# Cross-attention block on one core: the two copies of each next x tile moved to other places in the order of ScalarE and VectorE

## What is computed

```python
q = layer_norm(query, ln1_g, ln1_b)
qh, kh, vh = q @ wq + bq, context @ wk + bk, context @ wv + bv   # 16 heads of 32
scores = where(allowed, einsum('bqhd,bkhd->bhqk', qh, kh) / sqrt(32), -inf)   # causal
o = einsum('bhqk,bkhd->bqhd', softmax(scores), vh)
x = query + (o @ wo + bo)
h = layer_norm(x, ln2_g, ln2_b)
out = x + gelu(h @ w1 + b1) @ w2 + b2
```

## Time and profile before

| | us |
|---|---|
| median of 3 runs | 3094.44 |
| lowest, highest | 3094.41, 3095.11 |
| the profiled execution, its own time | 3096.19 |
| span of its trace | 3094.5 |
| mean granted clock of TensorE, share of full | 0.982 |

### The profile page before, as it was taken

The page is one execution under the profiler, slowest core; times in us unless marked ns, Lnnn a source line. Parts: engine busy times, 40 slices in busy tenths (PEclk is TensorE's granted clock), DMA queues, the critical chain, the costliest instruction groups (busy, mean ns, idle before and its releaser), DMA issues. The chain is left out here.

```text
span 3094.5 us, 52560 instructions
## 1 busy us (share of the span) xinstructions
PE 2965.2 (96%) x17576; PEld 2408.6 (78%) x17576; DVE 1520.4 (49%) x4100; ACT 1153.1 (37%) x2958; POOL 459.1 (15%) x432
## 2 busy tenths in 40 slices
PE   6999999999999999999979999999999999999999
PEld 5777877778777777777758888888888888888887
DVE  4766666666676666766634333322333322333322
ACT  3655566555666565655622111111111111111111
POOL 1222122211222112222112000000000000000000
PEclk9999999999999999999979999999999999999999
DMA  5766676666666666666522111100111100111100
GB/s 133 122 113 102 111 107 111 115 110 108 107 108 119 112 102 115 103 119 110 89 85 82 41 41 41 41 9 32 41 41 41 41 31 10 41 41 41 41 27 14
DMA packets 123695, 231.89 MB, mean 75 GB/s; under 512 B 10752, under 2 KB 10752, under 8 KB 123648
## 3 DMA queue, kind: packets, MB, share of 16 engines
q1 hardware_dynamic: 123648, 231.28, 37.5%
HBM read 97.02 MB, written 33.55 MB: 42 GB/s over the span
## 5 line engine op out<-in xcount | busy, mean ns | idle before, releaser
L710 ACT ACTIVATE sm<-sm,mins 128x128 f32<-128x128 f32 (+3 forms) x1024 | 571.7, 559 | 606.4 <-DVE mins L574 603.6
L574 DVE CUSTOM_DVE_ANT_0 sm<-bank_s,mask 128x128 f32<-128x128 f32 (+3 forms) x1024 | 480.7, 488 | 451.2 <-PE bank_s L425 440.5
L1146 ACT ACTIVATE g_sb<-bank_f,b1s 128x512 f32<-128x512 f32 x256 | 176.2, 688 | 1173.1 <-PE bank_f L956 1173.1
L1058 DVE CAST g_hi<-g_sb 128x512 fp32r<-128x512 f32 x256 | 113.0, 441 | 866.9 <-ACT g_sb L1146 866.9
L437 PE MATMUL bank_t<-ident,sm 128*128 128x128 f32 x2560 | 424.1, 281 | 53.5 <-ACT pT L520 34.1
L437 PEld LDWEIGHTS bank_t<-ident,sm 128*128 128x128 f32 x2560 | 305.8, 143 | 156.9 <-issue 76.6
L954 PE MATMUL bank_f<-hT_hi,w_hi 128*128 128x512 f32 x1024 | 407.6, 398 | 1.6 <-DVE hT_lo L1052 1.6
L954 PE MATMUL bank_o<-w_hi,g_hi 128*128 128x512 f32 x1024 | 408.0, 398 | 0.0
L956 PE MATMUL bank_f<-hT_hi,w_lo 128*128 128x512 f32 x1024 | 406.7, 397 | 0.0
L955 PE MATMUL bank_f<-hT_lo,w_hi 128*128 128x512 f32 x1024 | 406.4, 397 | 0.0
L956 PE MATMUL bank_o<-w_hi,g_lo 128*128 128x512 f32 x1024 | 406.3, 397 | 0.0
(11 more groups left out here) (108 smaller groups left out, 4486.5 us busy)
## 6 DMA issues: line engine op xcount, KB each, us to landing
stack<-st_hi SPq DMA_DIRECT2D x256, 256.0 KB, 5.6
xt<-in_x SPq DMA_DIRECT2D x32, 1024.0 KB, 5.3
stack<-st_lo SPq DMA_DIRECT2D x128, 256.0 KB, 7.2
c_raw<-in_ctxT SPq DMA_DIRECT2D x64, 256.0 KB, 6.0
x_scratch<-xt SPq DMA_DIRECT2D x64, 256.0 KB, 2.0
xn<-x_scratch SPq DMA_DIRECT2D x16, 1024.0 KB, 7.7
xr<-x_scratch SPq DMA_DIRECT2D x16, 1024.0 KB, 5.6
out<-xr SPq DMA_DIRECT2D x64, 256.0 KB, 2.1
```

The costliest lines, as they stand in the source:

```text
L574: op = V.tensor_tensor_reduce(sm[:, n % SLOTS_S, off:off + w], bank_s[n % BANKS_S][:, off:off + w], mask[:, 512 - w:512], 1.0, 0.0, ALU.ad ...
L710: op = A.activation(row, row, ACT.Exp, bias=mins[:, g % 2, c:c + 1], scale=-1.0, accum_out=sums[:, g % 2, c:c + 1])
L1058: V.tensor_copy(g_hi[:, f % RING_H, :], g_sb[:, f % 2, :]).then_inc(g_hi_ok, 1)
L1146: A.activation(g_sb[:, f % 2, :], bank_f[f % 2][:], ACT.Gelu, bias=b1s[:, f:f + 1], scale=1.0).then_inc(gelu, 1)
```

## The change

On ACT, `x_high` is called at the start of the step in which its X job ends, ahead of `exponential`, instead of behind exponential, move and `o_high`. On DVE, `x_low` is called right behind `mask_and_max` of the step in which the job ends, ahead of the move, instead of at the end of the following step. The conditions of the waits, the buffers and PE's order stay as they are. The prologue's four X tiles are not touched.

```diff
--- before.py
+++ after.py
@@ -627,6 +627,9 @@
                     g, k = divmod(n, TG)
                     if not it.tail:
                         mask_and_max(it, n)
+                    for job, jg in it.ended(n):
+                        if job[0] == "X":
+                            x_low(it, job, jg, it.b + 1)
                     if (n > LAG and not it.tail or n <= LAG and not it.first) and not act_moves((n - LAG - 1) % TG):
                         move_tile(dve, V.tensor_copy, it, n - LAG - 1)
                     beside_previous = g < NG and not (it.first and g == 0) and n < len(it.steps)
@@ -645,8 +648,6 @@
                                 normalise(it.b + 1, t)
                     for job, jg in it.ended(n - 1):
 
-                        if job[0] == "X":
-                            x_low(it, job, jg, it.b + 1)
                         if job[0] in "QK":
                             qk_low(it, job, jg, it.b * NG + (jg + 1))
                     for job, jg in it.ended(n):
@@ -742,6 +743,9 @@
             def body(it):
                 for n in range(len(it.steps)):
                     g, k = divmod(n, TG)
+                    for job, jg in it.ended(n):
+                        if job[0] == "X":
+                            x_high(it, job, jg)
                     if not it.tail:
                         exponential(it, n)
                     if (n > LAG and not it.tail or n <= LAG and not it.first) and act_moves((n - LAG - 1) % TG):
@@ -752,8 +756,6 @@
                         if k == (O_HIGH_LATE if g == 1 else O_HIGH_AT):
                             o_high(it, g - 1)
                     for job, jg in it.ended(n):
-                        if job[0] == "X":
-                            x_high(it, job, jg)
                         if job[0] in "QK":
                             qk_high(it, job, jg, it.b * NG + (jg + 1))
                         if job[0] == "V":
```

## The result

| | before | after |
|---|---|---|
| median, us | 3094.78 (4 runs, 3094.41 to 3096.00) | 3068.83 (4 runs, 3062.19 to 3069.66) |
| profiled execution, us | 3096.19 | 3068.40 |
| span, us | 3094.5 | 3066.7 |
| mean granted clock | 0.982 | 0.989 |

The ratio is 0.9911, with a 95% interval of 0.9894 to 0.9928: 26 us faster, where 13 were forecast.

What follows compares the result with a forecast made beforehand. PE was taken to bound the kernel except for some 9 us per batch, where DVE is the limit. 5.3 us from the shorter chain plus 7.7 from the clock gave 13.0: median 3081.4 from 3094.44, range 3066 to 3093.

Steps and rivals of the forecast that it cites:

- the clock: Behind PE's wait ahead of the Q product: 5 of 14 clock drops saved, 5 x 1.54 = 7.7 us.
- DVE is the limit in the x steps, PE elsewhere: Four x steps per stage A batch: DVE busy 9.08 of 9.40 us, PE 6.23; whole batches: PE 90.88 of 95.32.
- The chain of starts: Steps 7 to 11, worked out by start-to-start distances: Q product at 1449.42 instead of 1449.77.
- The gain per batch in the x steps: X3's wait goes, the wait for step 10's move takes nearly all its place: 0.35 per batch, 5.3 us in 15.
- The new wait for ScalarE's copy: DVE, step 10: waits 0.84 us for ACT's copy of X3, with the move of step 10 queued behind.
- The price of one: A drop from 2.4 to 1.2 GHz where PE is dense costs 1.54 us, from batches of 95.32 and 93.78.
- rival (a): Behind the Q product's wait the clock stays as it is: two close waits work like one, or only matmuls count; 3089.1, chance 0.23.
- Rival (b): Behind the Q product's wait all drops go, as a wait below 1 us never brings one; 3067.5, chance 0.17.
- Rival (c): Slower: a doubled wait before step 8's transposes brings a drop inside the x steps; up to 3112.2, chance 0.10.
- Rival (d): ACT holds up X3's copy 0.2 to 0.4 more, clock gives little: no effect that can be told; 3091 to 3096, chance 0.13.

Runs made afterwards that it cites:

- two kernels with filler: Kernel before, with six matmuls or twelve transposes of overwritten result added into PE's wait ahead of the Q product: 3076.17 and 3076.69 us beside 3095.81.
- kernel with VectorE's half alone: Changed kernel with ScalarE's copies back behind the exponential, only VectorE's low-half subtractions staying early: 3187.47 us, ratio 1.0291.
- four further orders: Changed kernel with VectorE's subtractions back: 3093.56; X3's low half back: 3105.84; step 10's move first: 3056.08; all low halves behind moves, ScalarE's step 9 move earlier: 3046.22.

## Why the prediction was right and wrong

The step that failed is one term of the sum, the clock: 7.7 us were forecast for it where some 20 came. The rest of the working held, in the parts below.

*DVE is the limit in the x steps, PE elsewhere: right.* With the same instructions, the order of VectorE's queue alone made the kernel before 92 us slower and the changed kernel another 13 us faster (3068.78 to 3056.08). One reading is loose but enters no term: of the four x steps only step 7 has a normalisation, and step 9 has no move on VectorE.

*The chain of starts: right within 0.13 us at each step.* Three waits of 1.22, 0.74 and 0.72 were worked out as 1.23, 0.75 and 0.83. The gain per batch in the x steps was worked out as 0.35 and is 0.42, 6.3 us instead of 5.3. The new wait for ScalarE's copy is there, 0.76 for 0.84.

*The sum that failed is the term of the clock.* The prediction put it as "I take 9 drops left, nearer to the rows with drops: 5 x 1.54 = 7.7 us". There were none left: 14 x 1.54 = 21.6, of which the 20.0 of thirteen drops show up to the last Q product. The price of one was right, as the two kernels with filler show; the number of drops was not. Two things were wrong in it. The idle time was taken as 1.58 where it is 1.46, since the last wait was overestimated by 0.11; and the only rows on either side were 1.71 and 0.84, so that "near to 1.71" was taken for "mostly drops", while batch 784, which had none with the full 1.71, was used only as an argument against rival (a). It said that 1.71 is itself close to the edge; read so, a shorter wait is rather free of drops. The kernel with one added matmul shows it: at 1.5 in one piece 12 of 15 batches were free of one in the profiled execution. Rival (b), all drops go, 3067.5, is what happened (3068.8); it had been given 0.17. Its reason, that a wait below 1 us never brings a drop, is not shown by that: the changed kernel also has a wait of 1.22 in each batch. And that its time is met within 1.3 us is partly luck, since the x steps gave 1.0 more than it has and about 2 us were given back behind the last batch.

*Rival (a) and the rule behind it: wrong.* The Trainium skill (TensorE: Matmul & The Clock Gate, Part 4: PE-mode transpose) says that transposes don't count as PE activity as matmuls do. Here twelve transposes in the wait kept the clock up as six matmuls did (3076.69 and 3076.17), so in this kernel the trace differs from the rule, and the measurement decides: transposes do count here, though how much of one counts is not shown. The first half of rival (a), two waits close together work like one, is not supported either: 0.74 and 0.72 brought no drop, one wait of 1.5 three in fifteen.

*Rival (c), a drop inside the x steps: didn't happen here.* It did in the kernel with VectorE's half alone: on PE the x steps shown for it above have waits of 3.18 and 2.75 us, and the stretch of 18 us around them has a mean clock of 0.73, with the drop inside them:

```profile
1423.00:1441.00 18.00, 12.08 (x71) 9.65 (x70) 11.22 (x30) 8.59 (x22) 8.69 (x9) 0.73 0.49 113
```

*Rival (d), the copy of X3 held up more: no.* It starts where the distances put it, 5.58 behind the maximum of step 7 (5.61).

## What to carry to other kernels

Where a short stretch makes a second engine the limit, replay that stretch by start-to-start distances of its rows: it gave four further orders within a few us here, and the harmful one as harmful (80 us and lost clock forecast, 92 measured). When work is put ahead in a queue, look at what it waits for: if that depends on what the same queue has just handed out, every instruction behind it waits for the round trip, so do the work that others wait for first. And a stall of PE ahead of dense work may cost nearly its length twice, once as a wait (1.71 us here) and once as half clock behind it (1.54); shortening or filling it so that the drop stays away pays even where the stall itself stays (20 us here).

## What was not expected of the hardware

- A stall of 1.71 us brought a drop in 14 of 15 batches, one of 1.5 in 3 of 15, one of 1.2 in none, and two of 0.74 and 0.72 with work between in none. From 1.71 to 1.5 us of idle time the kernel became 15 us faster (3095.77 to 3080.88).
- Useless matmuls or transposes made the kernel before 19 to 20 us faster.
- Twelve useless transposes did it as six matmuls did; two matmuls were enough too.
